# GpSimd waits, ahead of the eighth gather of a chunk, for the first seven gathers of that chunk to land

## The reference, cut to what matters

```python
h_fwd = layernorm(x) @ W_forward.T ; h_rev = layernorm(x) @ W_reverse.T
messages = h_fwd[src] * direction[:, 0:1] + h_rev[src] * direction[:, 1:2]
scores = leaky_relu(messages @ attn.T)                 # 4 heads
exp_scores = exp(scores - max)
norm = exp_scores / (segment_sum(exp_scores, dst)[dst] + 1e-10)
out[h] = segment_sum(messages * norm[:, h], dst)       # 64 features, 4 heads
x = x + out ; x = x + ffn(layernorm(x))                # gate, top 2 of 16 experts, layernorm
```

## Time and profile before

| What | Value |
|---|---|
| median of 3 timed runs | 2554.95 us (2554.32 to 2557.01) |
| span of the profiled execution | 2909.8 us |
| mean granted TensorE clock in it | 0.841 of full speed |
| busy: PE / DVE / POOL / ACT | 74% / 64% / 60% / 12% |
| gathers of the edge stage | 1375, 1027 ns each on the mean |

### The profile page before, as it was taken

How to read it: one execution, slowest core, us unless ns; L and a number is a source line. 1 busy time by engine, 2 the same in 40 slices (tenths; PEclk the granted TensorE clock), 3 DMA queues, 4 the chain that set the end, 5 groups by cost and what they waited for, 6 DMA issues and landing times.

```text
span 2909.8 us, 44243 instructions
## 1 busy us (share of the span) xinstructions
PE 2151.1 (74%) x11977; PEld 1813.9 (62%) x11978; DVE 1860.1 (64%) x4481; ACT 350.5 (12%) x936; POOL 1744.0 (60%) x1757
## 2 busy tenths in 40 slices
PE   6587877778877676877777776777763547999990
PEld 6466765666666565666666665566653446888880
DVE  6666666657666665666576666567664566666656
ACT  4000000000000000000000000000002433434444
POOL 6667666667666666666666666567663554333326
PEclk8698888878788898988798988889875558999995
DMA  5222222222222222222222222222224456656657
GB/s 185 54 53 56 50 50 50 52 51 53 50 51 48 50 53 53 50 51 51 50 50 55 53 53 50 49 50 56 50 46 126 136 184 186 205 193 194 198 166 266
DMA packets 176304, 256.65 MB, mean 88 GB/s; under 512 B 47078, under 2 KB 120999, under 8 KB 176004
## 3 DMA queue, kind: packets, MB, share of 16 engines
q0 software_dynamic: 53696, 121.60, 16.9%
q1 hardware_dynamic: 122564, 134.56, 15.2%
HBM read 218.11 MB, written 38.79 MB: 88 GB/s over the span
## 4 chain that ended last, share of the span: by engine, by line
PE 32%; DVE 26%; issue 17%; another core or an unknown queue 14%; DVEq 7%; DMA 2%; POOL 1%; ACT 1%; SPq 0%; ACTq 0%; POOLq 0%
PE p_hot L966 28%; DVE p_hot L1053 4%; DVE onehot L1043 3%; DVEq L1702 3%; DVE shared L985 2%; DVEq L869 2%; DVE p_part L993 2%; DVE hot_ex L1023 1%; PE p_y L1870 1%; DVE p_y L1925 1%; PE p_h L1860 1%; DVE rows L990 1%; PE p_win L878 1%; DVE second L1905 1%
## 5 line engine op out<-in xcount | busy, mean ns | idle before, releaser
L262 POOL DMA_INDIRECT rows<-node_table,index x1375 | 1411.7, 1027 | 742.4 <-issue 446.5
L966 PE MATMUL p_hot<-parts,onehot 128*128 128x476 f32 x5264 | 1379.7, 419 | 467.7 <-DVE onehot L1043 256.0
L966 PEld LDWEIGHTS p_hot<-parts,onehot 128*128 128x128 f32 x5264 | 1092.9, 210 | 725.3 <-issue 283.1
L1053 DVE SCALAR_TENSOR_TENSOR p_hot<-place_no,place_of_source,p_hot 128x476 f32<-128x476 f32 x376 | 250.7, 712 | 350.4 <-remote 291.3
L985 DVE TENSOR_TENSOR shared<-shared,p_win 65x64 f32 x784 | 170.9, 218 | 361.2 <-remote 258.7
L878 PE MATMUL p_win<-hot_ex,msg 128*65 128x64 f32 x3136 | 231.7, 237 | 75.5 <-DVE hot_ex L1023 58.4
L928 ACT ACTIVATE ex<-score,neg_shift 128x64 f32<-128x64 f32 x98 | 34.3, 350 | 2087.2 <-DVE score L1010 1824.7
L878 PEld LDWEIGHTS p_win<-hot_ex,msg 128*65 128x65 f32 x3136 | 226.2, 152 | 94.7 <-issue 86.4
L1711 POOL DMA_INDIRECT expert_rows<-ys,back x104 | 103.1, 992 | 269.3 <-DVE ys L1930 195.5
L1058 DVE TENSOR_REDUCE rows<-p_hot 128x136 f32<-128x952 f32 x188 | 216.0, 1149 | 6.5
L1860 PEld LDWEIGHTS p_h<-xt,shared 128*128 128x128 f32 x1664 | 198.1, 193 | 35.2 <-ACT xt L1802 29.8
(11 more groups left out here) (268 smaller groups left out, 1401.3 us busy)
## 6 DMA issues: line engine op xcount, KB each, us to landing
shared<-in_w SPq DMA_DIRECT2D x120, 512.0 KB
rows<-node_table,index POOLq DMA_INDIRECT x1375
xs<-dispatched SPq DMA_DIRECT2D x104, 129.5 KB
key<-hot_keys SPq DMA_DIRECT2D x94, 128.0 KB
shared<-expert_rows SPq DMA_DIRECT2D x12, 896.0 KB, 8.6
token_rows<-in_x SPq DMA_DIRECT2D x7, 896.0 KB
shared<-in_x SPq DMA_DIRECT2D x7, 768.0 KB
out<-shared SPq DMA_DIRECT2D x6, 896.0 KB, 7.5
```

Source lines behind the costliest of these rows:

```text
L262: pool.indirect_dma_start(out=rows[:, s, k, :], out_offset=None, in_=table, in_offset=bass.IndirectOffsetOnAxis(ap=index[:, s, 0, k:k + 1] ...
L966: last = pe.matmul(p_hot[:, j, d, 0:PLACES * COLS], onehot[:, j, gr, :], parts[:, gr:NT:GP, m, d * COLS:(d + 1) * COLS], start=(gr == 0 an ...
L1053: last = dve.scalar_tensor_tensor(out=found[:, d], in0=place_no[:, :].unsqueeze(2).broadcast_to([P, PLACES, COLS]), scalar=place[:, ds(f, ...
```

## The change

Ahead of gather 7 of a chunk (the eighth) POOL now also waits until `gathered[s]` has reached the count of this chunk's first seven gathers. The count is exact: `KG * it` gathers of the earlier chunks of this buffer and 7 of this one. Chunk 1, whose first eight gathers were issued before the loop, is left out (`begun`). The waits of `summed`, `score_ready` and `msg_ready` stay as they are, and so do all gathers.

```diff
                     after(pool, summed, c - 1)
                     settle(pool, turns)
                     piece(1, 7)
+                    if not begun:
+                        pool.wait_ge(gathered[s], 16 * (KG * it + 7))
                     pool.wait_ge(score_ready, c)
                     settle(pool, turns)
                     piece(7, 11)
```

## The result

The changed kernel takes 2760.49 us (median of 4 runs, 2759.75 to 2761.36) against 2555.24 (4 runs) for the kernel before: 205 us more, a ratio of 1.0802 with a 95% interval of 1.0787 to 1.0817. The forecast was 2734 us, with 2630 to 2785 as its range; the wait costs what was said, a little more each time.

The account below looks back on a forecast made before the run. The prediction took POOL's issuing of gathers to bound the edge stage in timed runs: 96 waits at 1.5 + 0.66 - 0.30 = 1.86 us make 179 us, and 2555 + 179 = 2734 us, range 2630 to 2785.

Parts of the forecast that it names:

- What bounds a timed run: Edge stage: POOL's issuing of gathers bounds timed runs; span 2909.8 less 329 us of POOL waits gives 2581, near 2555.
- Partly absorbed: Rival: 70 us of POOL's waits remain in a timed run and take up delay, leaving 109 us, 2664; chance 0.15.
- absorbed: Rival: timed runs hold POOL's waits as profiled, so only DVE's slack counts; about 2565 us; chance 0.12.
- The count: One new wait in each chunk from 2 to 97, 96 in all.
- The price: Ahead of the eighth gather: each wait costs 1.5 + 0.66 - 0.30 = 1.86 us (1.36 to 2.26).
- Landing: At the new wait: the seventh gather lands 1.5 us behind its recorded end, at least 1.0.
- Starting again: POOL's restart after the semaphore: 0.66 us, from one semaphore that let POOL go 0.66 us later than DVE.
- Nothing gives it back: After the wait gathers go on at 1.25 us each, so DVE's start of each chunk moves by the full 1.86.
- The faster case: Rival: the gather behind the wait avoids stretching beside `hot_ex`, saving up to 0.74 us a chunk; 2522 us; chance 0.05.
- What the profile would show: About 2.2 us idle ahead of eighth gathers, idle total up under 179, line 990 waiting, span growing less than the median.

Follow-up runs that it names:

- second profile: The kernel before, unchanged, run and profiled once more: 2551.59 us, ratio 0.9992, with a profiled span of 2549.7 us.
- without the pacing waits: The kernel before without POOL's waits for window sums (`summed`), scores (`score_ready`) and messages (`msg_ready`), the buffer wait kept: 2554.15 us, ratio 1.0001.
- the met wait: The changed kernel with its new wait only for gathers of earlier chunks of the same buffer, which landed long ago: 2553.81 us, ratio 0.9999.
- first profile: The kernel before, unchanged, in the profiled execution that the prediction read: span 2909.8 us, against a timed median of 2555 us.

## Why the prediction was right

*What bounds a timed run.* Right, and the step on which all depended: the span of the profile less POOL's waits (2581) came near the timed median, so a timed run couldn't hold these waits. The second profile shows 31 us of them, and the run with a gather fewer gains 146 us. Partly absorbed (2664) and absorbed (2565) are both out. That the sum met the median to 26 us was in part luck. Of the 360 us between the two profiled spans 299 are idle ahead of the gathers (742.4 less 443.6). Some 60 that the sum left out lie in shorter gathers (1411.7 against 1391.7) and behind the start of the last gather (697.7 against 657.6), and it took off 31 us of idle that stay.

*The count.* 96 waits were forecast, and 96 stand in the trace.

*The price.* 1.86 us forecast, 2.16 found; this term was too small, and 96 × 0.30 = 29 us is about what lies between 2734 and 2760. Both parts fall short, as far as a landing known to a tenth can tell. Landing: 2.6 us from issue less 0.94 on POOL is 1.66 behind the gather's end, where the stores of the earlier trace rows had given 1.5. Starting again: 2.46 - 1.66 = 0.80, where the comparison with DVE had given 0.66. That comparison leaves out DVE's own start: in the rows above, line 992 starts 1036.92 - 1034.21 = 2.71 us after the issue of the chunk's last gather, 0.1 behind a landing of 2.6. That is a hint and not shown, since landings spread from 2.5 to 3.7. By the estimate from the Trainium skill, DMA: Bandwidth & Descriptors ("Anatomy of one DMA — SWDGE (gpsimd) path"), a gather lands 2.16 us after issue; the trace has 2.6, and the measurement decides.

*Nothing gives it back.* Right: a second wait costs the same again, and without the pacing waits the time doesn't change.

*The faster case.* Out: the wait costs three times what a stretched gather could save, and the mean gather is as long after (1011 ns) as in the second profile of before (1012).

*What the profile would show.* The idle ahead of the eighth gather (2.2 forecast, 2.46 found) and line 990's waiting for gathers came as said. The idle total of the gathers was to grow by less than 179 us, because the idle ahead of the second gather would shrink; against the second profile it grew by 206 (443.6 to 650.0), since a usual execution has no such idle to shrink. That the profiled span would grow much less than the timed median was said of an execution like the first one; the changed kernel's profile wasn't of that kind, so this was not seen.

## What to carry to other kernels

Where a profiled span and the timed runs differ by more than what is to be decided, subtract one engine's waits from the span and see which remainder meets the timed median: that engine is the first candidate for the bound, even if the chain of the profile gives it 1%, and a second profile can confirm it. A wait of an engine for a transfer that it has only just issued costs the way to landing and the engine's own start again, here 2.16 us a wait with only 0.3 us of moving data in it; one more gather issued in between took its own 1.25 us off, and two made the wait free. Other sizes of transfer were not tried. Ahead of such a wait ask how many instructions lie between the last issue that it counts and the wait itself.

## What was not expected of the hardware

POOL lost time once in 112 gathers, 12 times in a run: 2.1 to 2.2 us of idle that waited for nothing in the trace, ahead of the second gather of each eighth chunk, and a longer gather behind it (1.56 us). The loss is there in the kernel before, with the met wait, without pacing, in the changed kernel and with two waits; it is missing where the gathers of a chunk count on two semaphores in place of one, or where a chunk has 13 gathers. So it hangs neither on the waits nor on the number of instructions alone, and is worth 1% of this kernel. It isn't the fetching of instructions either: from 136 to 1830 us of the second profile, with 11 of the losses, the DMA queues for instructions moved a single packet. What it is stays open.

In the first profile POOL waited for PE's semaphores, and there are stretches in which PE issued one matmul in 1.4 to 2.8 us, as from 1142 to 1161:

```profile
1145.13 0.38 PE L966 MATMUL p_hot<-parts,onehot 128*128 128x476 f32 x1 [2.42 <-issue]
1147.93 0.56 PE L966 MATMUL p_hot<-parts,onehot 128*128 128x476 f32 x1 [2.42 <-issue]
```

No other profile here shows that. Its cause is open too.
